# One graph, attention and expert layer on one core: the order of 40 fetches behind 40 spills, and the distances of a group of edges made by one difference and one square instead of eight squares

## The reference

```python
x = h @ W;  el = x @ Wl.T;  er = x @ Wr.T          # h: layer norm of the nodes; 4 heads
e = jnp.exp(leaky_relu(el[src] + er[dst], 0.2))
rowsum = segment_sum(e, src)
heads = [segment_sum((e / rowsum[src])[:, hd:hd+1] * x[dst], src) for hd in range(4)]
out = elu(stack(heads) + b)
```

## Time and profile before

| | |
|---|---|
| median of 3 runs | 2994.3 us (2986.27 to 2997.49) |
| profiled execution, its own time | 2988.45 us |
| its span, first to last instruction | 2986.6 us |
| busy: PE, DVE, ACT, POOL | 1888.2, 2065.1, 1868.2, 1825.2 us |

### The profile page before, as it was taken

The page is one execution under the profiler, slowest core; times in us unless marked ns, Lnnn a source line. Parts: engine busy times, 40 slices in busy tenths (PEclk is TensorE's granted clock), DMA queues, the critical chain, the costliest instruction groups (busy, mean ns, idle before and its releaser), DMA issues.

```text
span 2986.6 us, 48066 instructions
## 1 busy us (share of the span) xinstructions
PE 1888.2 (63%) x8550; PEld 1584.1 (53%) x8551; DVE 2065.1 (69%) x4596; ACT 1868.2 (63%) x6576; POOL 1825.2 (61%) x1826
## 2 busy tenths in 40 slices
PE   1763365157676667888887665655656562478993
PEld 0331332046566666777776555555555552367772
DVE  8988688866677667888887666665655656844453
ACT  1443343177678778999998666666666664654541
POOL 0004788877777777437777777777777750444453
PEclk8786677555555555555555555555555555589996
DMA  9011211133323332111111111111111115234664
GB/s 322 8 12 33 52 41 30 45 100 89 89 74 89 89 87 77 53 35 28 28 29 28 28 29 28 28 28 28 29 28 29 28 22 144 85 116 155 191 200 135
DMA packets 159838, 206.71 MB, mean 69 GB/s; under 512 B 47107, under 2 KB 117051, under 8 KB 159490
## 3 DMA queue, kind: packets, MB, share of 16 engines
q0 software_dynamic: 60992, 82.75, 12.8%
q1 hardware_dynamic: 91408, 115.05, 11.8%
q10 hardware_dynamic: 7346, 7.92, 0.9%
HBM read 124.08 MB, written 74.97 MB: 67 GB/s over the span
## 4 chain that ended last, share of the span: by engine, by line
POOL 52%; issue 18%; PE 12%; DVE 8%; ACT 7%; DMA 2%; ACTq 1%; SPq 0%; POOLq 0%; DVEq 0%
POOL arena L1665 51%; PE ps L1310 4%; PE ps L1326 3%; DVE arena L699 2%; DVE arena L700 2%; ACT arena L1496 1%; PE ps L1131 1%; ACT arena L1485 1%; PE ps L1318 1%; PE ps L1302 1%; ACT arena L1474 1%; ACT ps L1475 1%; PE ps L1234 1%; POOL arena L1688 1%; PE ps L1262 1%
## 5 line engine op out<-in xcount | busy, mean ns | idle before, releaser
L1665 POOL DMA_INDIRECT arena<-gather_table,arena x1612 | 1620.9, 1006 | 821.2 <-issue 488.0
L1234 PE MATMUL ps<-arena 128*128 x4784 | 1097.4, 421 | 387.8 <-DVE big L888 382.4
L1234 PEld LDWEIGHTS ps<-arena 128*128 128x128 f32 x4784 | 1042.8, 330 | 454.2 <-issue 453.9
L864 DVE TENSOR_TENSOR ps<-ps,arena 128x512 f32<-128x512 f32 x598 | 388.0, 694 | 388.6 <-ACT arena L1491 323.6
L1496 ACT ACTIVATE arena<-lane,arena 128x32 f32<-128x32 f32 x2392 | 536.4, 311 | 0.0
L1485 ACT ACTIVATE arena<-arena 128x2 f32 x1196 | 254.3, 286 | 418.4 <-SPq L1774 251.5
L877 DVE TENSOR_TENSOR arena<-ps,arena 128x1024 f32<-128x1024 f32 x299 | 365.9, 1224 | 117.7 <-ACT ps L1475 117.6
L872 DVE TENSOR_TENSOR ps<-ps,arena 128x1024 f32<-128x1024 f32 x299 | 367.6, 1229 | 36.3 <-ACT arena L1496 35.9
L1224 PE MATMUL ps<-el,pick_w 48*128 x1196 | 204.6, 294 | 221.2 <-issue 166.6
L1474 ACT ACTIVATE arena<-ps 128x1024 f32<-128x1024 f32 x299 | 302.4, 1011 | 62.1 <-issue 61.4
L1475 ACT ACTIVATE ps<-ps 128x1024 f32<-128x1024 f32 x299 | 302.7, 1012 | 0.0
(11 more groups left out here) (292 smaller groups left out, 1898.5 us busy)
## 6 DMA issues: line engine op xcount, KB each, us to landing
arena<-gather_table,arena POOLq DMA_INDIRECT x1612, 2.4
staged_rows<-arena SPq DMA_DIRECT2D x40, 552.0 KB, 2.8
arena<-staged_rows SPq DMA_DIRECT2D x40, 552.0 KB, 5.1
arena<-slot_rows SPq DMA_DIRECT2D x119, 128.0 KB, 2.2
expert_rows<-arena SPq DMA_DIRECT2D x119, 128.0 KB, 2.7
slot_rows<-ends_w SPq DMA_DIRECT2D x2, 4480.0 KB, 25.5
arena<-big SPq DMA_DIRECT2D x112, 56.9 KB
slot_rows<-ends_w SPq DMA_DIRECT2D x1, 6272.0 KB, 33.1
```

Source lines behind the costliest of these rows:

```text
L864: ins = dve.tensor_tensor(z5[:, :, c, :, :], row, bcast(er[:, :, c, :], 3, WN), ALU.add)
L1234: ins = pe.matmul(ps[:, 6 + u % 2, i * AW:i * AW + AW], share_w[u % 4][:, (i * GT + c) * P:(i * GT + c + 1) * P], gat[:, bass.ds(place["ag ...
L1665: pool.indirect_dma_start(rows, None, table_d, bass.IndirectOffsetOnAxis(ap=dst_x[:, t:t + 1], axis=0)).then_inc(s_gat[p % LAND], 16)
```

## The change

Two edits. In SyncE's order, the turn at which each fetch stands is now a table: fetches 0 to 3 where they were (turns 10 to 13), and from there 40 fetches for 29 turns, so that fetch 37 stands behind spill 38, fetch 38 behind spill 39 and fetch 39 behind all. In the groups, VectorE makes the difference of lane and `loc` for all 8 x 32 elements in one instruction, and ScalarE squares the result in place in one instruction.

```diff
-    STAGE, STAGES, AHEAD = 8, 3, 10
+    STAGE, STAGES = 8, 3
+    FETCH_AT = [10 + n if n < 4 else 14 + (n - 3) * 29 // 40 for n in range(NST)]
...
-            step(dve.tensor_scalar(window, window, float(WN) * FAR, None, ALU.mult), "tables")
+            step(dve.tensor_scalar(window, window, -float(WN), None, ALU.mult), "tables")
...
+            def distances(g, u):
+                par = u % 2
+                dve.wait_ge(s_loc, g + 1)
+                after(dve, s_zsub, g, 2)
+                dve.tensor_tensor(away[par], bcast(lane[:, 0:WN], 1, GS), bcast(loc[par][:, :], 2, WN), ALU.subtract).then_inc(s_dist, 1)
...
-                for i, (part, lag) in enumerate(((add_ers, 1), (put_away, 1), (weigh, 2))):
+                for i, (part, lag) in enumerate(((add_ers, 1), (distances, 0), (put_away, 1), (weigh, 2))):
...
-                        for q in ((0,), (1,), (2, 3))[i]:
+                        for q in ((0,), (), (1,), (2, 3))[i]:
...
+                after(act, s_dist, g, 2)
...
-                                         bias=bases[:, sl(g * GI + i)], scale=-FAR)
+                                         bias=bases[:, sl(g * GI + i)])
...
-                act.wait_ge(s_loc, g + 1)
-                after(act, s_zsub, g, 2)
-                for j in range(GS):
-                    ins = act.activation(away[par][:, j, :], lane[:, 0:WN], ACT.Square, bias=loc[par][:, j:j + 1], scale=FAR)
-                ins.then_inc(s_away, 1)
+                act.wait_ge(s_dist, g + 1)
+                act.activation(away[par], away[par], ACT.Square, scale=FAR).then_inc(s_away, 1)
...
-            for n in range(NST + AHEAD):
+            for n in range(max(NST, FETCH_AT[-1] + 1)):
...
-                if n >= AHEAD:
-                    fetch(n - AHEAD)
+                for q in range(NST):
+                    if FETCH_AT[q] == n:
+                        fetch(q)
```

More of the change, by code:

```diff
@@ L401, in gps_layer @@
         s_loc = sem("s_loc")
+        s_dist = sem("s_dist")
         s_away = sem("s_away")
```

## The result

The changed kernel takes 2974.68 us (median of 4 runs, 2973.95 to 2978.52) against 2992.23 us before (4 runs, 2986.27 to 2997.49): a ratio of 0.9945, 95% interval 0.9923 to 0.9966. That is 17.6 us less, and the interval makes it 10 to 23. The profiled execution took 2975.23 us, its span is 2973.4; against 2988.45 us that is 13.2 us less.

What follows compares the result with a forecast made beforehand. GpSimd's gathers, restarting late behind the staged pairs, were taken to set the end. 42 us from the restart, less 18 for held gathers, plus 1 at the tail, gave 25 us saved: 2969, given as 2970, range 2945 to 3000.

Steps and rivals of the forecast that it cites:

- the restart: GpSimd's start of pair 352, after its idle wait: at 1269 us instead of 1310.68, 42 us saved.
- the tail: The last group's chain behind the last gather: about 1 us shorter.
- The bound: GpSimd's gathers: what moves their restart of 1310.68 us moves the end, if their pace behind it stays 1.25 us.
- VectorE becomes the limit: Groups catching up: VectorE replaces ScalarE as limit, 5.03 us a group for 4.87, with a 1.6 us loop turn each fourth.
- the rival of a longer group: VectorE's group exceeds 5.03 us, through waiting for `loc` or a costlier loop turn; at 0.2 us more, 2988 us; chance 0.16.
- The 13th group: Aggregation of the 13th group: ends at 701 us for 697.8 before, an estimated 3 us later.
- The pace: The 96 groups up to fetch 37: 5.03 us each, putting that fetch at 1184 us.
- What the difference does to the gathers: VectorE's difference, both inputs in SBUF, holds GpSimd's gathers: 137 groups at 0.11 us plus 3 us, together 18 us.
- groups at a random phase: 47 groups not locked to the gathers' period: 0.07 us each, 3 us.
- the dear rival: A blocked gather waits for most of 0.41 us; 184 groups cost 75 us, end at 3026 us; chance 0.14.
- The gathers do mind: Against the rival that the difference does not delay gathers: gain 43 us, 2951 us; chance 0.20.
- The groups did not outrun the spills: Rival: VectorE hides its loop turn, 4.63 us a group, spill 39 stays at 1155.3 us, 2939 us; chance 0.08.

Runs made afterwards that it cites:

- run 2: The kernel of run 1 with eight squares as before the change, so SyncE's new fetch order (40 for 29 turns) alone: 2947.24 us, ratio 0.9867.
- run 8: The kernel of run 1 with the difference made twice in each group, first into a place nothing reads: 3019.04 us, ratio 1.0103.
- run 4: The kernel of run 1 with all four of ScalarE's copies of attention terms ahead of `loc`: 2984.83 us, ratio 0.9987.
- run 7: The kernel of run 1 with two of ScalarE's four copies of attention terms ahead of `loc`: 2973.87 us, ratio 0.9945.
- run 10: The kernel of run 6 with two of ScalarE's four copies of attention terms ahead of `loc`: 2924.23 us, ratio 0.978.
- run 5: The kernel of run 1 with eight squares as before the change and 40 fetches for 32 turns: 2918.77 us, ratio 0.977.
- run 9: The kernel of run 6 with one of ScalarE's four copies of attention terms ahead of `loc`: 2930.97 us, ratio 0.9802.
- run 6: The kernel of run 1 with 40 fetches for 32 turns in place of 29: 2941.27 us, ratio 0.984.
- run 1: The changed kernel with one more register operation, altering no value, on each value ScalarE and SyncE wait for in the groups: 2984.41 us, ratio 0.9981.

## Why the prediction was nearly right, step by step

2970 was forecast and 2974.68 measured, inside the range and inside the forecast's own 2959 to 2981. The direction and the chain of causes held; several terms were off, and two of them offset each other. The gain forecast was 25 us; the medians give 17.6 and the two traced executions 13.2. In these executions the restart gave 16.4 us less than forecast, the gathers cost 6.5 less, and the tail was 1.9 the other way. That the time came out within 5 us is in part luck: one error hid some of another, and the medians lie 4.3 us further apart than the executions in which the terms can be read.

**The bound.** Right. GpSimd's restart behind the staged pairs sets the end: run 2, which changes only SyncE's order, gives 42 us and moves the last gather by 40.6.

**VectorE becomes the limit.** Right. Groups start 4.55 us apart with the difference in its place between the first sum and `put_away` (forecast 4.63), and the loop turn shows as 1.67 us idle (forecast 1.6); four groups take 1334.30 - 1314.31 = 20.0 us (forecast 20.1). From 720 to 1180 us there are 1804/92 = 19.6 groups per 100 us (forecast 19.9), with VectorE 87% busy, not 93, and ScalarE 69%:

```profile
1014.59 1.29 DVE L867 TENSOR_TENSOR ps<-ps,arena 128x512 f32<-128x512 f32 x2
1015.78 0.21 DVE L897 TENSOR_TENSOR big<-ps,big 128x65 f32 x1
1015.91 0.42 DVE L874 TENSOR_TENSOR arena<-lane,arena 128x256 f32<-128x256 f32 x1
1016.25 1.23 DVE L881 TENSOR_TENSOR ps<-ps,arena 128x1024 f32<-128x1024 f32 x1
...
1019.14 1.29 DVE L867 TENSOR_TENSOR ps<-ps,arena 128x512 f32<-128x512 f32 x2
...
1314.31 1.30 DVE L867 TENSOR_TENSOR ps<-ps,arena 128x512 f32<-128x512 f32 x2 [1.67 <-issue]
...
1334.30 1.30 DVE L867 TENSOR_TENSOR ps<-ps,arena 128x512 f32<-128x512 f32 x2 [1.67 <-issue]
```

The difference does not wait for `loc` in this stretch, so the rival of a longer group did not come about in that form.

**The restart, 42 us forecast, 25.6 measured.** This is the term that was mis-sized, in two of its parts. *The 13th group* ended at 704.26 + 3.67 = 707.9 us and not at 701. Of those 6.9 us, 3.4 are the whole program being later (spill 14 at 658.56 for 655.17), which no count of the change could give; the rest I had under-estimated. *The pace* from there to fetch 37 was (1198.34 - 707.93)/96 = 5.11 us and not 5.03, outside the 5.00 to 5.07 that the forecast allowed. VectorE does starve now and then, where I had let it run at its own limit throughout: from 708 to 1198 us it waits four times for ScalarE's terms, 14.0 us in all. Of the 24 loop turns only 20 show as idle time, so each of these waits stands in the place of a turn of 1.67 us. Timelines of the changed kernel: the difference waiting near the 13th group, the 13th aggregation, then two of four waits for ScalarE's terms:

```profile
700.78 0.43 DVE L874 TENSOR_TENSOR arena<-lane,arena 128x256 f32<-128x256 f32 x1 [6.23 <-ACT arena L1495]
...
704.26 3.67 PE L1243 MATMUL ps<-arena 128*128 x16 [4.57 <-DVE big L897]
...
887.85 1.30 DVE L867 TENSOR_TENSOR ps<-ps,arena 128x512 f32<-128x512 f32 x2 [3.37 <-ACT arena L1501]
969.89 1.30 DVE L867 TENSOR_TENSOR ps<-ps,arena 128x512 f32<-128x512 f32 x2 [3.53 <-ACT arena L1501]
```

Together, 6.9 + 7.5 = 14.4 us: fetch 37 at 1198.34 for 1184, spill 39 at 1199.04 for 1185. Pair 320 stands 5.84 us behind that, where 3.8 was taken (1204.88 for 1189), and pair 352 so at 1285.07 for 1269. That a stop at pair 352 would vanish was right, and so was that its idle time would come back as a late pair 320. Run 8 confirms the lever, 96 groups on spill 39, to within 1 us of 32.

**What the difference does to the gathers, 18 us forecast, 11.5 measured.** That the difference holds gathers, and that the price hangs on its phase, was right and is the best supported point: runs 4, 7 and 10 move the difference and all but 0.6 to 2.8 us of the loss goes, runs 2 and 5 have none. Timelines of the changed kernel:

```profile
2007.08 0.43 DVE L874 TENSOR_TENSOR arena<-lane,arena 128x256 f32<-128x256 f32 x1 [2.86 <-ACT arena L1495]
2007.36 0.97 POOL L1672 DMA_INDIRECT arena<-gather_table,arena  x1 [0.30 <-issue]
...
2014.66 0.43 DVE L874 TENSOR_TENSOR arena<-lane,arena 128x256 f32<-128x256 f32 x1 [1.17 <-ACT arena L1495]
2014.87 1.04 POOL L1672 DMA_INDIRECT arena<-gather_table,arena  x1 [0.31 <-issue]
```

The mean of a held gather, 12.5/130 = 0.10 us, is close to the 0.11 forecast. The 3 us for groups at a random phase did not come: from pair 320 to 1440 us 3 gathers were held, for 0.35 us, and from 600 to 1160 us 8, for 0.6 us. Phase need not be random there, since four groups take 20.0 us and so do 16 gathers, and the pattern repeats. The width of the window was wrong, the row's 0.41 for 0.24 us; it did not hurt the sum, because the end of the hold, which sets the price, was right (the difference's end + 0.81, here forecast as 0.83). But it bears on the dear rival: no gather beside the groups paid more than 0.27 us (1.21 for 0.944) in any trace here, so 184 groups at 0.41, 75 us, did not come near. Its point of decision, 0.23 us a group, is a price that only the few gathers at the edge paid.

The Trainium skill, SBUF — State Buffer, section "Who interferes with whom", infers that a VectorE instruction with two inputs in SBUF does not stall the making of a gather's descriptors. If that is taken to cover a gather whose row numbers lie in SBUF, as here, the runs show otherwise: 1.19 us for 0.94 when the difference starts 0.05 us ahead, none when it starts 0.04 us ahead or later. No run tells whether the reading of the row numbers or the making of the descriptors is what waits; the first would fit the section's other statement, that such an instruction contends with GpSimd's reads. The section's rule of full blocking agrees with the hold of some 0.24 us for 256 elements and 0.12 for 128, and with run 9, where the one that comes second waits.

**The tail.** 1 us less was forecast, 0.9 us more measured.

**The rivals.** The gathers do mind, and not most of 0.41 us. A group longer than 5.03 us came half true, through starving and not through `loc`. The groups did not outrun the spills at 29 for 40; at 32 for 40 they did (run 6), because SyncE then asks for less.

**What the change was worth by parts.** The fetches' order gives 42 us (run 2, 2989.4 to 2947.2). The edit in the groups takes 37 of it (run 1, 2984.4), some 15 at the restart and 20 in the gathers. In the changed kernel itself, without the added operation, 17.6 us are left, so there it takes some 25. The best forms are run 5, 2918.77 us, and run 10, 2924.23 us, whose intervals overlap; even where no gather is held, one difference and one square gain nothing over eight squares. At 29 for 40 they move the limit from ScalarE to VectorE at nearly the same height (5.05 and 5.10 us a group); at 32 for 40 the groups are hardly waited for: from 700 to 1160 us SyncE's queue waits 389.9 us for gathered rows and 15.8 for the groups in run 5, 345.0 and 70.0 in run 10.

## What to carry to other kernels

Test the two edits of a change apart before adding them: here one gives 42 us and the other takes 25 to 37 of it back. When a queue's written order feeds a slower consumer, ask for no more than the consumer can take (16 us a stage and not 14.5), or the overdue waits will stand ahead of what others need. And when a periodic engine shares something with another, place the short instruction by its phase: 0.13 us of delay by an instruction moved ahead was worth 10 us here, and eight squares that never touch GpSimd cost nothing.

## What the runs showed of the hardware that was not expected

- A VectorE difference of 128x256 with both inputs in SBUF holds a gather if it starts 0.28 to 0.05 us ahead of it, until 1.24 us after its own start; at 0.04 us ahead it holds nothing. With 128x128 the end is at 1.11 us.
- The wait goes both ways: a difference that starts from 0.04 us ahead of a gather to 0.02 behind is itself longer, up to 0.50 us for 0.43, and ends 0.45 to 0.47 us after the gather's start (run 9).
- GpSimd gets its turn between two such instructions that stand back to back (run 8), so their holds do not add up.
- One register operation ahead of each wait moved this phase enough to raise the held time from 12.5 to 19.4 us and the median from 2974.68 to 2984.41 us, measured in two sets of runs whose kernels before stand at 2992.23 and 2989.36 us.
